# The middle stage's attention values with the value matrix as TensorE's weights: two heads of a pair in the two halves of its columns, and 1/sum spread by TensorE

## The chip, the cores and the metric

One NeuronCore of a Trainium2 chip runs the whole kernel. The metric is the device time of one execution in microseconds. The kernel before has a median of 1403.51 us over three executions (1403.35 to 1405.44).

## The reference

For 16 batches of 112 tokens (width 256) and 375 context tokens, two gated layers of attention and feed-forward follow each other. The change touches the second attention ("large heads", 16 heads of 64) alone:

```
q = ln(x) @ Wq;  k, v = split(concat([ln(ctx), ln(x)]) @ Wkv)       # 112 queries, 487 keys
weight = softmax(where(mask, q k^T / 8, -max))                       # per head, 112 x 487
out = weight @ v                                                     # per head, 112 x 64
x = x + tanh(g) * (out as 112 x 1024) @ Wout
```

After it come a layer norm, a router that picks two of eight experts for each token, and the experts' feed-forward.

## The kernel before

The program has three stages, one after the other: small heads and a first feed-forward (to about 484 us), large heads (`phase_attention_large_heads`, to about 1194 us), and the experts. Products are made in three fp16 passes (`PASSES`: high by high, high by low, low by high) of operands that are split into a high and a low half, so each logical matrix product is three matmuls.

The middle stage runs 16 bodies, one for each batch `b`, of 16 steps `s`. Every engine has its own program with the same steps, and semaphores tie them. Work of several batches lies in one body:

- `scores`: at steps 0, 1, 3, ... 13 PE makes the scores of two heads (six matmuls, which alternate between the two halves of PE's rows; the first pair at step 0). DVE adds the mask and takes the minimum (`maxima`, L1808), ACT makes the exponential with its row sum (L1682) and then the fp16 high half (L1707), and DVE for even heads (L1813) and POOL for odd ones (L1315) subtract to get the low half.
- SP turns a head's `halves` into `pT` (keys on partitions) with a transposing DMA (`turn`, L1236), three steps after the head. `pT` and `halves` have room for `TURN` = 8 heads.
- `values` (L1601): at each step PE multiplies one head, `LAG` = 5 steps behind. The weights are a 128x112 block of probabilities (four blocks of keys; read as 128 columns), the moving operand is the head's 64 columns of `v_s`, so the output is queries by head columns in `ps_o`, eight heads to a bank, 12 matmuls a head.
- `item`: the products for the next batch, one at each step (L1493): eight of keys (`k_s`, six matmuls of 487 columns), eight of values (`v_s`, six of 512 columns), and two of queries (24 of 112 columns). They alternate between two PSUM banks; ACT copies the high half and DVE subtracts for the low half, and an item waits until the one before the last is read.
- One more bank, `ps_x`, is lent by step (`XSLOT`, `lend`): to the previous batch's tail (`h`), to the transposes of the batch after next (`n`), to the router's ranks (`r`) and to the query items (`q`). Each tenant waits until the one before has been read.

The tail of a batch before the change: `out_heads` on DVE takes the reciprocals of eight heads' sums and multiplies a bank of `ps_o` by them (L1823) into `o_n`; `hitem` 0 and 1 are four fp32 transposes each into `ps_x` (L1536), an ACT copy to the high half of `oT` (L1675) and a DVE subtraction for the low half (L1829). Then comes the product with `Wout` (`H_O`, 24 matmuls of 256 columns), the norm, the transposes `H_X` and the router's `H_G`. In the step of a body PE's order is: scores, item, what `XSLOT` has, values.

## Time and profile before

| | us |
|---|---|
| median of three executions | 1403.51 |
| the profiled execution | 1406.79 |
| its span, in which the trace counts | 1405.0 |
| PE, DVE, ACT, POOL busy | 1225.0, 1083.2, 999.4, 813.3 |

Engines: PE is TensorE's matmuls and PEld its weight loads, DVE is VectorE, ACT ScalarE, POOL GpSimd, SP SyncE. A row's matmuls last longer than the distance between their starts, since they are pipelined, so PE's work is read here as the time from the start of one group to the start of the next.

### The profile page before, as it was taken

To read this page: it belongs to the slowest core of one execution; us is meant where nothing else is said; L and a number is where in the kernel's file an instruction comes from. 1 tells how busy PE (TensorE), PEld (TensorE's weight loads), DVE (VectorE), ACT (ScalarE), POOL (GpSimd) and SP (SyncE) were. 2 spreads that over 40 slices of the span, in tenths; PEclk is the share of its full clock that TensorE was granted. 3 is DMA by queue.
4 is the path that set the end of the run, shared out by engine and by line. 5 is a ranking of instruction groups with operands and counts; after the bars stand their busy time and mean duration, and the time that the engine had idled before them with its cause. 6 is when DMAs were issued, how large, how long until landed. Compare 5 with 4: busy or idle time off the path is not lost. (4 is left out here: it accounts for less than half of the span.)

```text
span 1405.0 us, 38066 instructions
## 1 busy us (share of the span) xinstructions
PE 1225.0 (87%) x13060; PEld 880.3 (63%) x13060; DVE 1083.2 (77%) x3112; ACT 999.4 (71%) x2552; POOL 813.3 (58%) x1204
## 2 busy tenths in 40 slices
PE   3999999999986499999999999999999974489994
PEld 1777777777764245566656566656666653389894
DVE  3799999999985168888888888888888882477872
ACT  2888888888883358877787887787888771256562
POOL 3544444444454346677777777777777674146564
PEclk7799999999987599999999999999999985699997
DMA  5444545455420148877788777878777793854333
GB/s 162 131 146 144 148 120 169 114 151 155 134 50 7 49 94 156 141 147 146 153 158 160 143 146 154 147 151 163 152 144 152 137 196 61 316 154 60 57 36 76
DMA packets 309406, 185.50 MB, mean 132 GB/s; under 512 B 257930, under 2 KB 295186, under 8 KB 306112
## 3 DMA queue, kind: packets, MB, share of 16 engines
q1 hardware_dynamic: 293024, 140.82, 47.3%
q0 software_dynamic: 13168, 35.80, 10.5%
q10 hardware_dynamic: 3024, 6.47, 1.5%
q8 instruction: 106, 1.74, 0.5%
q14 instruction: 84, 0.69, 0.2%
HBM read 76.19 MB, written 49.94 MB: 90 GB/s over the span
## 5 line engine op out<-in xcount | busy, mean ns | idle before, releaser
L1682 ACT ACTIVATE b_prob<-b_prob,b_top 112x487 f32<-112x487 f32 x256 | 178.9, 699 | 28.3 <-DVE b_top L1808 26.5
L1315 POOL TENSOR_TENSOR b_halves<-b_prob,b_halves 112x487 f16<-112x487 f32 x128 | 146.9, 1148 | 83.7 <-ACT b_halves L1707 82.2
L1493 PE MATMUL b_ps_p<-w_s,b_tok_s 128*128 128x512 f16 (+1 forms) x768 | 187.7, 381 | 4.0 <-DVE b_k_s L1795 3.2
L1493 PE MATMUL b_ps_p<-b_tok_s,w_s 128*128 128x487 f16 x768 | 181.9, 374 | 6.6 <-POOL b_tok_s L1309 3.7
L1808 DVE CUSTOM_DVE_ANT_0 b_prob<-b_ps_s,b_keep 112x487 f32<-112x487 f32 x256 | 167.3, 655 | 13.2 <-PE b_ps_s L1586 11.6
L717 ACT ACTIVATE a_prob<-a_prob,a_top 112x375 f32<-112x375 f32 x256 | 154.8, 605 | 3.7 <-DVE a_top L853 2.0
L1707 ACT ACTIVATE b_halves<-b_prob 112x487 f16<-112x487 f32 x256 | 156.0, 609 | 0.6
L853 DVE CUSTOM_DVE_ANT_0 a_prob<-a_ps_s,a_keep 112x375 f32<-112x375 f32 x256 | 138.1, 540 | 21.7 <-PE a_ps_s L610 21.4
L618 PE MATMUL a_ps_t<-a_const,a_prob 112*125 112x112 f32 x768 | 135.7, 287 | 10.6 <-ACT a_prob L717 9.1
L1601 PEld LDWEIGHTS b_ps_o<-b_v_s,b_pT 128*128 128x128 f16 (+1 forms) x3072 | 123.9, 99 | 31.4 <-DMA b_pT<-b_halves 11.6
L1601 PE MATMUL b_ps_o<-b_v_s,b_pT 128*128 128x64 f16 (+1 forms) x3072 | 135.0, 195 | 9.2 <-DMA b_pT<-b_halves 9.1
L858 DVE TENSOR_TENSOR a_pT<-a_ps_t,a_pT 125x336 f16<-125x336 f32 x256 | 128.1, 500 | 19.2 <-ACT a_pT L724 18.7
L618 PEld LDWEIGHTS a_ps_t<-a_const,a_prob 112*125 112x125 f32 x768 | 117.5, 196 | 36.1 <-ACT a_prob L717 28.1
L1493 PEld LDWEIGHTS b_ps_p<-b_tok_s,w_s 128*128 128x128 f16 x768 | 66.0, 98 | 95.1 <-issue 20.3
L1493 PEld LDWEIGHTS b_ps_p<-w_s,b_tok_s 128*128 128x128 f16 (+1 forms) x768 | 70.7, 105 | 83.5 <-DVE b_k_s L1795 12.5
L1795 DVE TENSOR_TENSOR b_k_s<-b_ps_p,b_k_s 128x487 f16<-128x487 f32 x128 | 84.5, 661 | 49.9 <-ACT b_k_s L1663 49.9
L1813 DVE TENSOR_TENSOR b_halves<-b_prob,b_halves 112x487 f16<-112x487 f32 x128 | 120.9, 945 | 0.0
L724 ACT ACTIVATE a_pT<-a_ps_t 125x336 f16<-125x336 f32 x256 | 113.5, 443 | 2.3 <-PE a_ps_t L618 2.2
L1670 ACT ACTIVATE b_v_s<-b_ps_p 128x512 f16<-128x512 f32 (+1 forms) x128 | 76.2, 595 | 53.1 <-PE b_ps_p L1493 52.1
L1803 DVE TENSOR_TENSOR b_v_s<-b_ps_p,b_v_s 128x512 f16<-128x512 f32 (+1 forms) x128 | 87.9, 686 | 31.7 <-ACT b_v_s L1670 31.7
L1586 PE MATMUL b_ps_s<-b_k_s,b_q_s 64*112 64x487 f16 x768 | 107.1, 385 | 0.3 <-DVE b_top L1808 0.3
L1663 ACT ACTIVATE b_k_s<-b_ps_p 128x487 f16<-128x487 f32 x128 | 72.8, 570 | 41.6 <-PE b_ps_p L1493 40.2
(263 smaller groups left out, 3022.9 us busy)
## 6 DMA issues: line engine op xcount, KB each, us to landing
xs<-a_blank SPq DMA_DIRECT2D x14, 1032.0 KB, 4.5
c_w_pool<-w_split SPq DMA_DIRECT2D x8, 1600.0 KB, 10.6
b_wch_f<-in_w_experts POOLq DMA_DIRECT2D x32, 384.0 KB, 5.2
w_split<-b_wch_s POOLq DMA_DIRECT2D x32, 384.0 KB, 3.9
a_k_stack<-keys SPq DMA_DIRECT2D x96, 93.8 KB, 3.1
a_ctx_f<-in_ctxT SPq DMA_DIRECT2D x16, 375.0 KB, 3.8
keys<-a_k_s SPq DMA_DIRECT2D x16, 375.0 KB, 3.2
b_ctx_t<-in_ctx SPq DMA_DIRECT2D x16, 375.0 KB
```

Source lines behind the costliest of these rows:

```text
L618: last = pe.transpose(ps_t[h % 2][0:KB0, j * T:(j + 1) * T], prob[:, h % RING, j * KB0:(j + 1) * KB0], ident[0:T, 0:T])
L717: act.activation(prob[:, h % RING, :], prob[:, h % RING, :], ACT.Exp, bias=top[:, h % RING:h % RING + 1], scale=-1.0, accum_out=sums[par][ ...
L724: act.activation(pT[0:KB0, h % RING, HI, :, 0:T], ps_t[h % 2][0:KB0, 0:NB0 * T].rearrange("p (j n) -> p j n", j=NB0), ACT.Copy).then_inc(s ...
L853: dve.tensor_tensor_reduce(prob[:, h % RING, :], ps_s[h % 2][0:T, 0:C], keep[par][:, :], -SCALE0, 3e38, ALU.add, ALU.min, top[:, h % RING: ...
L858: dve.tensor_tensor(pT[0:KB0, h % RING, LO, :, 0:T], ps_t[h % 2][0:KB0, 0:NB0 * T].rearrange("p (j n) -> p j n", j=NB0), pT[0:KB0, h % RIN ...
L1315: pool.tensor_tensor(halves[:, h % TURN, LO, 0:NK], prob[:, h % RING, 0:NK], halves[:, h % TURN, HI, 0:NK], ALU.subtract).then_inc(s_lo[1], 1)
L1493: last = pe.matmul(out, sta(a, k), mov(m, k), start=(k == 0 and n == 0), stop=(k == tiles - 1 and n == 2))
L1601: last = pe.matmul(ps_o[h // 8][:, col:col + D1], pT[0:k, h % TURN, a, j, :], v_s[par][0:k, m, j, h * D1:(h + 1) * D1], start=(h % 8 == 0 ...
L1682: act.activation(prob[:, h % RING, 0:NK], prob[:, h % RING, 0:NK], ACT.Exp, bias=top[:, h % RING:h % RING + 1], scale=-1.0, accum_out=sums ...
L1707: act.activation(halves[:, h % TURN, HI, 0:NK], prob[:, h % RING, 0:NK], ACT.Copy).then_inc(s_hi, 1)
L1808: dve.tensor_tensor_reduce(prob[:, h % RING, 0:NK], ps_s[h % 3][0:T, 0:NK], keep[par][:, :], -SCALE1, 3e38, ALU.add, ALU.min, top[:, h % R ...
L1813: dve.tensor_tensor(halves[:, h % TURN, LO, 0:NK], prob[:, h % RING, 0:NK], halves[:, h % TURN, HI, 0:NK], ALU.subtract).then_inc(s_lo[0], 1)
```

## The change

`values` now takes a pair of heads at each even step, `PAIRLAG` = 6 steps behind. The weights are a head's 128x64 block of `v_s`, the moving operand is the 112 columns of `pT`. The even head is written to partitions 0 to 63 of `ps_o`, then the odd head to 64 to 127, so a bank holds four pairs, already turned (head columns on partitions, queries in the columns). The four-matmul transposes of `o_n` go away. In their place the reciprocals of eight heads are transposed (`H_T`, one transpose to 8x112), scaled by 4096 and split by DVE in two small instructions (`rT`), and multiplied by a 0/1 matrix `picks` (`H_B`, eight matmuls with 8 rows and 112 columns) so that each partition gets its head's reciprocal; ACT copies that to `r_f`; DVE multiplies `ps_o` by it into `o_f`. ACT makes the high half of `oT` from `o_f` (`out_high`), POOL the low half (`out_low`). `XSLOT` has two more slots, 0 and 15. `FREED` counts the semaphore's value after each tail item, since `H_T` raises it twice. The renamed counts in other waits are left out of the diff.

```diff
@@ -1002,7 +1002,8 @@
 KLAST = NK - (NB1 - 1) * KB1
-LAG = 5
+PAIRLAG = 6
+WHOLE = 4096.0
@@ -1059,12 +1060,15 @@
         halves = sb("halves", [T, TURN, 2, NB1 * KB1], F16)
-        pT = sb("pT", [128, TURN, 2, NB1, 128], F16)
+        pT = sb("pT", [128, TURN, 2, NB1, T], F16)
...
         rsum = sb("rsum", [T, H], F32)
-        o_n = sb("o_n", [T, H, D1], F32)
+        picks = sb("picks", [8, 4, 128], F16)
+        rT = sb("rT", [8, 2, T], F16)
+        r_f = sb("r_f", [128, 4 * T], F32)
+        o_f = [sb(f"o_f{i}", [128, 4 * T], F32) for i in range(2)]
@@ -1091,6 +1095,7 @@
         order = sb("order", [T, T], F32)
+        aim = order[0:8, 0:8].rearrange("p (j n) -> p j n", j=4)
@@ -1172,9 +1177,13 @@
-        H_T, H_O, H_X, H_G, HI_ = 0, 2, 3, 4, 5
+        H_T, H_B, H_O, H_X, H_G, NH = (0, 2), (1, 3), 4, 5, 6, 7
+        FREED = (2, 3, 5, 6, 7, 8, 9)
+        HF = FREED[-1]
+        A_B, A_O, AH = (1, 3), (2, 4), 5
         ROUTE = 7
-        NCONST2 = 6
+        NCONST2 = 8
@@ -1184,8 +1193,8 @@
-        XSLOT = {1: ("h", 0), 2: ("r", 0), 3: ("q", 0), 4: ("q", 1), 6: ("h", 1), 8: ("n", 0), 9: ("h", 2), 10: ("n", 1), 11: ("n", 2),
-                 13: ("h", 3), 14: ("h", 4)}
+        XSLOT = {0: ("h", H_B[0]), 1: ("h", H_T[1]), 2: ("r", 0), 3: ("q", 0), 4: ("q", 1), 5: ("h", H_B[1]), 8: ("n", 0), 9: ("h", H_O),
+                 10: ("n", 1), 11: ("n", 2), 13: ("h", H_X), 14: ("h", H_G), 15: ("t", H_T[0])}
@@ -1222,18 +1231,18 @@
...
-                need_all(sp, settled, (s_lo[h % 2], H // 2, b, h // 2 + 1), (s_pv, H, b, h - TURN + 1),
+                need_all(sp, settled, (s_lo[h % 2], H // 2, b, h // 2 + 1), (s_pv, H // 2, b, (h - TURN) // 2 + 1),
                          (s_turned[h % RING], 16 * (H // RING), b, 16 * (h // RING)))
-                sp.dma_start(pT[:, h % TURN, :, :, 0:T].rearrange("p s j n -> p (s j) n"),
+                sp.dma_start(pT[:, h % TURN, :, :, :].rearrange("p s j n -> p (s j) n"),
@@ -1270,9 +1279,8 @@
             pool.memset(halves[:, :, :, NK:NB1 * KB1], 0.0).then_inc(s_zero, 1)
-            pool.memset(pT[:, :, :, :, T:128], 0.0).then_inc(s_zero, 1)
@@ -1315,12 +1323,23 @@
+            def out_low(c, i):
+                need(pool, s_hhi, AH, c, A_O[i], settled)
+                pool.tensor_tensor(oT[:, LO, 4 * i:4 * i + 4, :], o_f[i][:, :].rearrange("p (j n) -> p j n", j=4), oT[:, HI, 4 * i:4 * i + 4, :],
+                                   ALU.subtract).then_inc(s_olo, 1)
...
+                pool.iota(aim, [[2, 4], [1, 2]], base=0, channel_multiplier=-1, allow_small_or_imprecise_dtypes=True).then_inc(s_const2, 1)
+                pool.wait_ge(s_const2, 1)
+                pool.tensor_scalar(picks[:, :, :].rearrange("p j (o n) -> p j o n", o=2), aim.unsqueeze(3).to_broadcast([8, 4, 2, 64]),
+                                   0.0, None, ALU.is_equal).then_inc(s_const2, 1)
+                pool.wait_ge(s_const2, 2)
...
                 pool.iota(token[:, :], [[0, 1]], base=0, channel_multiplier=1, allow_small_or_imprecise_dtypes=True).then_inc(s_const2, 1)
-                pool.wait_ge(s_const2, 3)
+                pool.wait_ge(s_const2, 5)
@@ -1443,6 +1462,8 @@
                     if not first(b):
+                        if s in (3, 7):
+                            out_low(b - 1, s // 7)
@@ -1530,21 +1553,27 @@
             def hitem(c, k):
-                if k < H_O:
-                    for n in range(4):
-                        j = 4 * k + n
-                        last = pe.transpose(ps_x[:, n * T:(n + 1) * T], o_n[:, 2 * j:2 * j + 2, :].rearrange("p h d -> p (h d)"), ident[0:T, 0:T])
+                if k in H_T:
+                    i = H_T.index(k)
+                    need(pe, s_rsum, 2, c, i + 1)
+                    last = pe.transpose(ps_x[0:8, 0:T], rsum[:, 8 * i:8 * i + 8], ident[0:T, 0:T])
+                elif k in H_B:
+                    if first(c):
+                        pe.wait_ge(s_const2, NCONST2)
+                    for j in range(4):
+                        for part in (HI, LO):
+                            last = pe.matmul(ps_x[:, j * T:(j + 1) * T], picks[:, j, :], rT[:, part, :], start=(part == HI), stop=(part == LO))
                 elif k == H_O:
-                    need(pe, s_hhi, 3, c, 2)
-                    need(pe, s_hfree, HI_, c, 2)
+                    need(pe, s_hhi, AH, c, A_O[1])
+                    need(pe, s_olo, 2, c, 2)
@@ -1556,7 +1585,7 @@
                 if not first(b):
-                    need(pe, s_hfree, HI_, b - 1, nh)
+                    need(pe, s_hfree, HF, b - 1, FREED[nh])
@@ -1566,9 +1595,9 @@
                 elif kind == "h":
-                    if k < H_O:
-                        need(pe, s_oread, 2, b - 1, k + 1)
                     hitem(b - 1, k)
+                elif kind == "t":
+                    hitem(b, k)
@@ -1587,21 +1616,24 @@
-            def values(b, par, h):
-                need(pe, s_turned[h % RING], 16 * (H // RING), b, 16 * (h // RING + 1))
-                if h == 0:
+            def values(b, par, pair):
+                for h in (2 * pair, 2 * pair + 1):
+                    need(pe, s_turned[h % RING], 16 * (H // RING), b, 16 * (h // RING + 1))
+                if pair == 0:
...
                     need(pe, s_ifree, PI, b, PI)
-                if h % 8 == 0:
-                    need(pe, s_oread, 2, b - 1, h // 8 + 1)
-                col = (h % 8) * D1
-                for j in range(NB1):
-                    k = rows_of(j)
-                    for n, (a, m) in enumerate(PASSES):
-                        last = pe.matmul(ps_o[h // 8][:, col:col + D1], pT[0:k, h % TURN, a, j, :],
-                                         v_s[par][0:k, m, j, h * D1:(h + 1) * D1],
-                                         start=(h % 8 == 0 and j == 0 and n == 0),
-                                         stop=(j == NB1 - 1 and n == 2), skip_group_check=True)
+                if pair % 4 == 0:
+                    need(pe, s_hfree, HF, b - 1, FREED[H_B[pair // 4]])
+                cols = slice((pair % 4) * T, (pair % 4 + 1) * T)
+                for half in range(2):
+                    h = 2 * pair + half
+                    for j in range(NB1):
+                        k = rows_of(j)
+                        for n, (a, m) in enumerate(PASSES):
+                            last = pe.matmul(ps_o[pair // 4][64 * half:64 * half + 64, cols], v_s[par][0:k, m, j, h * D1:(h + 1) * D1],
+                                             pT[0:k, h % TURN, a, j, :], start=(pair % 4 == 0 and j == 0 and n == 0),
+                                             stop=(j == NB1 - 1 and n == 2), skip_group_check=True)
@@ -1624,11 +1656,12 @@
                         lend(b, par, s)
-                    if not (first(b) and s < LAG):
-                        values(*behind(s, LAG, b, par))
+                    if s % 2 == 0 and not (first(b) and s < PAIRLAG):
+                        c, p, h = behind(s, PAIRLAG, b, par)
+                        values(c, p, h // 2)
@@ -1640,17 +1673,17 @@
             run_batches(pe, body)
-            for h in range(H - LAG, H):
-                values(B - 1, 1, h)
-            need(pe, s_hfree, HI_, B - 1, 0)
+            need(pe, s_hfree, HF, B - 1, FREED[0])
+            hitem(B - 1, 1)
+            for pair in range((H - PAIRLAG) // 2, H // 2):
+                values(B - 1, 1, pair)
+            need(pe, s_hfree, HF, B - 1, FREED[1])
@@ -1665,17 +1698,22 @@
...
             def hitem(c, k):
-                if k < H_O:
-                    need(act, s_hitem, HI_, c, k + 1)
-                    act.activation(oT[:, HI, 4 * k:4 * k + 4, :], ps_x[:, 0:4 * T].rearrange("p (j n) -> p j n", j=4), ACT.Copy).then_inc(s_hhi, 1)
+                if k in H_B:
+                    need(act, s_hitem, NH, c, k + 1)
+                    act.activation(r_f[:, :], ps_x[:, 0:4 * T], ACT.Copy).then_inc(s_hhi, 1)
+            def out_high(c, i):
+                need(act, s_hfree, HF, c, FREED[H_B[i]])
+                need(act, s_hitem, NH, c - 1, H_O + 1)
+                act.activation(oT[:, HI, 4 * i:4 * i + 4, :], o_f[i][:, :].rearrange("p (j n) -> p j n", j=4), ACT.Copy).then_inc(s_hhi, 1)
@@ -1732,6 +1770,8 @@
                         normalise(b + 2)
+                    if not first(b) and s in (2, 7):
+                        out_high(b - 1, s // 7)
@@ -1767,13 +1807,16 @@
             weigh(B - 2)
-            for k in range(HI_):
+            for i in range(2):
+                hitem(B - 1, H_B[i])
+                out_high(B - 1, i)
+            for k in range(H_O, NH):
@@ -1813,36 +1856,41 @@
-            def out_heads(c, par, i):
+            def shares(c, par, i):
...
                 need(dve, s_exp, H, c, 8 * i + 8)
+                need(dve, s_hitem, NH, c - 1, H_T[i] + 1)
                 dve.reciprocal(rsum[:, heads], sums[par][:, heads]).then_inc(s_rsum, 1)
-                need(dve, s_rsum, 2, c, i + 1)
-                need(dve, s_pv, H, c, 8 * i + 8)
-                need(dve, s_hitem, HI_, c - 1, i + 1)
-                dve.tensor_tensor(o_n[:, heads, :], ps_o[i][0:T, :].rearrange("p (h d) -> p h d", h=8),
-                                  rsum[:, heads].unsqueeze(2).to_broadcast([T, 8, D1]), ALU.mult).then_inc(s_oread, 1)
...
             def hitem(c, k):
-                if k < H_O:
-                    need(dve, s_hhi, 3, c, k + 1)
-                    dve.tensor_tensor(oT[:, LO, 4 * k:4 * k + 4, :], ps_x[:, 0:4 * T].rearrange("p (j n) -> p j n", j=4), oT[:, HI, 4 * k:4 * k + 4, :], ALU.subtract).then_inc(s_hfree, 1)
+                if k in H_T:
+                    need(dve, s_hitem, NH, c, k + 1)
+                    dve.tensor_scalar(rT[:, HI, :], ps_x[0:8, 0:T], WHOLE, None, ALU.mult).then_inc(s_hfree, 1)
+                    need(dve, s_hfree, HF, c, FREED[k] - 1)
+                    dve.scalar_tensor_tensor(rT[:, LO, :], ps_x[0:8, 0:T], WHOLE, rT[:, HI, :], ALU.mult, ALU.subtract).then_inc(s_hfree, 1)
+                elif k in H_B:
+                    i = H_B.index(k)
+                    need(dve, s_hitem, NH, c, k + 1)
+                    need(dve, s_olo, 2, c - 1, i + 1)
+                    need(dve, s_hhi, AH, c, A_B[i])
+                    need(dve, s_pv, H // 2, c, 4 * i + 4)
+                    dve.scalar_tensor_tensor(o_f[i][:, :], ps_o[i][:, 0:4 * T], 1.0 / WHOLE, r_f[:, :], ALU.mult, ALU.mult).then_inc(s_hfree, 1)
@@ -1885,27 +1933,27 @@
                             item(b + 1, 1 - par, k)
-                    kind, k = XSLOT.get(s - 1, ("", 0))
+                    kind, k = XSLOT.get((s - 1) % H, ("", 0))
...
                         item(b + 1, 1 - par, ITEMS.index((kind, k)))
-                    if kind == "h" and not first(b):
+                    if kind in ("h", "t") and not first(b):
...
                     if not first(b):
-                        if s == 5:
-                            out_heads(b - 1, 1 - par, 1)
+                        if s == 0:
+                            shares(b - 1, 1 - par, 1)
...
                             norm_x3(b - 1)
-                    if s == 14:
-                        out_heads(b, par, 0)
+                    if s == 10:
+                        shares(b, par, 0)
@@ -1914,11 +1962,13 @@
             run_batches(dve, body)
+            hitem(B - 1, H_T[0])
...
             combine_weights(B - 2)
+            shares(B - 1, 1, 1)
+            hitem(B - 1, H_B[0])
             ranks(B - 2)
-            out_heads(B - 1, 1, 1)
-            for k in range(H_X):
+            for k in range(H_T[1], H_X):
...
```

## Rows read from the trace of the kernel before

**Rows 1.** Windows: one body, the last body, the tail. Length, busy of PE, PEld, DVE, ACT, POOL; PE clock; DMA share; GB/s.
```profile
798.00:840.00 42.00, 40.84 (x440) 25.64 (x436) 34.92 (x88) 34.00 (x81) 31.43 (x51) 1.00 0.82 150
...
1132.00:1172.00 40.00, 25.86 (x342) 19.13 (x338) 28.15 (x72) 23.34 (x54) 28.18 (x51) 0.76 0.91 176
1172.00:1184.00 12.00, 6.72 (x31) 5.86 (x31) 2.57 (x7) 0.90 (x2) 3.93 (x7) 0.64 0.10 29
```

**Rows 2.** Timeline of PE through one body: start us, length us, engine, line, what, count.
```profile
801.12 1.41 PE L1493 MATMUL b_ps_p<-b_tok_s,w_s 128*128 128x487 f16 x6 [0.20 <-DVE b_v_s L1803]
802.37 0.55 PE L1536 MATMUL b_ps_x<-b_const,b_o_n 112*128 112x112 f32 x4
802.75 0.52 PE L1601 MATMUL b_ps_o<-b_v_s,b_pT 128*128 128x64 f16 x12
803.11 1.40 PE L1493 MATMUL b_ps_p<-b_tok_s,w_s 128*128 128x487 f16 x6
805.23 0.21 PE L1613 MATMUL b_ps_x<-b_both,b_before 112*112 112x8 f16 x1 [0.72 <-DVE b_oT L1829]
...
805.36 0.51 PE L1601 MATMUL b_ps_o<-b_v_s,b_pT 128*128 128x64 f16 x12
805.80 0.83 PE L1586 MATMUL b_ps_s<-b_k_s,b_q_s 64*112 64x487 f16 x6
806.56 1.41 PE L1493 MATMUL b_ps_p<-b_tok_s,w_s 128*128 128x487 f16 x6
807.80 1.36 PE L1493 MATMUL b_ps_x<-b_tok_s,w_s 128*128 128x112 f16 x24
809.00 0.52 PE L1601 MATMUL b_ps_o<-b_v_s,b_pT 128*128 128x64 f16 x12
809.36 1.40 PE L1493 MATMUL b_ps_p<-b_tok_s,w_s 128*128 128x487 f16 x6
...
822.32 1.47 PE L1493 MATMUL b_ps_p<-w_s,b_tok_s 128*128 128x512 f16 x6
823.63 2.78 PE L1493 MATMUL b_ps_x<-w_s,b_oT 128*112 128x256 f16 x24
826.25 0.52 PE L1601 MATMUL b_ps_o<-b_v_s,b_pT 128*128 128x64 f16 x12
...
837.05 0.44 PE L1493 MATMUL b_ps_x<-b_wr_s,b_x3T 128*112 128x8 f16 x6
837.35 0.51 PE L1601 MATMUL b_ps_o<-b_v_s,b_pT 128*128 128x64 f16 x12
...
842.94 0.38 PE L1493 MATMUL b_ps_p<-b_tok_s,w_s 128*128 128x487 f16 x1 [0.20 <-DVE b_v_s L1803]
```

**Rows 3.** Timeline of PE, 0.1 us inside one group of six score matmuls.
```profile
812.24 0.62 PE L1586 MATMUL b_ps_s<-b_k_s,b_q_s 64*112 64x487 f16 x4
```

**Rows 4.** Timeline of PE and DVE around step 0 of a body.
```profile
798.41 1.41 PE L1493 MATMUL b_ps_p<-b_tok_s,w_s 128*128 128x487 f16 x6
...
798.52 0.67 DVE L1808 CUSTOM_DVE_ANT_0 b_prob<-b_ps_s,b_keep 112x487 f32<-112x487 f32 x1 [0.59 <-PE b_ps_s L1586]
...
799.11 1.36 DVE L1813 TENSOR_TENSOR b_halves<-b_prob,b_halves 112x487 f16<-112x487 f32 x1
...
799.66 0.52 PE L1601 MATMUL b_ps_o<-b_v_s,b_pT 128*128 128x64 f16 x12
...
800.39 0.68 DVE L1803 TENSOR_TENSOR b_v_s<-b_ps_p,b_v_s 103x512 f16<-103x512 f32 x1
```

**Rows 5.** Groups by line and shape, 620 to 1150 us: busy us, mean ns, idle before.
```profile
L1315 POOL TENSOR_TENSOR b_halves<-b_prob,b_halves 112x487 f16<-112x487 f32 x102 | 116.6, 1143 | 50.3 <-ACT b_halves L1707 49.1
...
L1813 DVE TENSOR_TENSOR b_halves<-b_prob,b_halves 112x487 f16<-112x487 f32 x103 | 98.0, 951 | 0.0
...
L1829 DVE TENSOR_TENSOR b_oT<-b_ps_x,b_oT 128x448 f16<-128x448 f32 x26 | 16.0, 615 | 0.3 <-ACT b_oT L1675 0.3
...
L1675 ACT ACTIVATE b_oT<-b_ps_x 128x448 f16<-128x448 f32 x26 | 13.9, 533 | 0.0
```

More of the change, by code:

```diff
@@ L1210, in _ @@
         def _(sp):
-            settled = (s_zero, 8)
+            settled = (s_zero, 7)
             def load_tokens(c):
@@ L1478, in _ @@
             send_rows(B - 2)
+            for i in range(2):
+                out_low(B - 1, i)
             deviation3(B - 1)
@@ L1545, in hitem @@
                 else:
-                    need(pe, s_hhi, 3, c, 3)
-                    need(pe, s_hfree, HI_, c, H_X + 1)
+                    need(pe, s_hhi, AH, c, AH)
+                    need(pe, s_hfree, HF, c, FREED[H_X])
                     last = product(ps_x[0:T, 0:E], lambda a, t: x3T[:, a, t, :], lambda a, t: wr_s[:, a, t, :])
@@ L1642, in _ @@
             run_batches(pe, body)
-            for h in range(H - LAG, H):
-                values(B - 1, 1, h)
-            need(pe, s_hfree, HI_, B - 1, 0)
+            need(pe, s_hfree, HF, B - 1, FREED[0])
[3 more added lines that the diff above has]
+            need(pe, s_hfree, HF, B - 1, FREED[1])
             ranks(B - 2)
             need(pe, s_rank, 1, B - 1, 0)
-            for k in range(HI_):
-                if k < H_O:
-                    need(pe, s_oread, 2, B - 1, k + 1)
-                need(pe, s_hfree, HI_, B - 1, k)
+            for k in range(2, NH):
+                need(pe, s_hfree, HF, B - 1, FREED[k - 1])
                 hitem(B - 1, k)
-            need(pe, s_hfree, HI_, B, 0)
+            need(pe, s_hfree, HF, B, 0)
             ranks(B - 1)
@@ L1667, in item @@
                     j, half = n // 2, n % 2
-                    need(act, s_pv, H, c - 1, 0)
+                    need(act, s_pv, H // 2, c - 1, 0)
                     r = rows_of(j)
@@ L1769, in _ @@
             weigh(B - 2)
-            for k in range(HI_):
+            for i in range(2):
+                hitem(B - 1, H_B[i])
+                out_high(B - 1, i)
+            for k in range(H_O, NH):
                 hitem(B - 1, k)
@@ L1775, in _ @@
         def _(dve):
-            settled = (s_zero, 8)
+            settled = (s_zero, 7)
             def stats(c):
@@ L1834, in hitem @@
                     dve.scalar_tensor_tensor(x3[:, :], ps_x[0:T, 0:D], tanhs[0:T, 1:2], x_res[:, :], ALU.mult, ALU.add).then_inc(s_hfree, 1)
-                    need(dve, s_hfree, HI_, c, k + 1)
+                    need(dve, s_hfree, HF, c, FREED[k])
                     dve.bn_stats(bns3[:, :], x3[:, :]).then_inc(s_stats3, 1)
@@ L1906, in body @@
                             stats(b + 2)
-            dve.wait_ge(s_zero, 8)
+            dve.wait_ge(s_zero, 7)
             stats(0)
```

25 lines of the change are left out of this document (12 added, 13 removed).

## The prediction

> **What bounds the kernel now.** I read the page first for the shares of the engines, then windows of one body each, then PE's timeline through a body, because a share of busy time doesn't say which engine sets the pace. In the windows the reader is to see that a body of the middle stage has PE busy for all but about 1 us at full clock, and DVE, ACT and POOL for 35, 34 and 31 of 42 us [rows 1]. In the timeline he is to see that PE's groups follow each other with hardly a gap. From one body's first product to the next body's is 842.94 - 801.12 = 41.82 us [rows 2]. Add up what PE has to issue in it, each as the distance to the next start: eight key products of 1.24, eight value products of 1.31, two query items of 1.20, eight groups of scores of 0.76, sixteen heads of values of 0.36 (and 0.08 more for the eight that scores follow: 0.44), the output product 2.62, two groups of output transposes of 0.38, the router 0.30 [rows 2]. That is 9.92 + 10.48 + 2.40 + 6.08 + 5.76 + 0.64 + 2.62 + 0.76 + 0.30 = 38.96. The short groups that are left (five, none longer than the 0.38 of the output transposes) I put at 1.2. So about 40.2 us are work and 1.6 are gaps. The largest is at the ranks: the product at 803.11 is through at 804.35, the ranks start at 805.23, so 0.88 us in which PE waits for DVE's read of `ps_x`. PE sets the pace of bodies 0 to 14. What lengthens PE's issue lengthens the kernel, and what is taken from DVE is worth something only in those 1.6 us.
>
> The last body has no products for a next batch. There PE is busy 25.9 of 40 us at a mean clock of 0.76 and the DMA engines 0.91 [rows 1], so PE doesn't set the pace there.
>
> **The values themselves.** Before, a head is 12 matmuls with 64 moving columns, and takes 0.36 us, 30 ns each [rows 2]. After, it is still 12, but 112 columns move. The row for that width is the query item: 24 matmuls of 112 columns in 1.20 us, 50 ns each [rows 2]. A pair then takes 24 x 0.050 = 1.20 instead of 0.72: +0.48 us. The two heads come one after the other, each twelve matmuls accumulate in one half, so I count no overlap but the last against the first.
>
> Are the weight loads hidden? A group with 8 moving columns and loads of 112 columns takes 0.30 us for six, 50 ns each [rows 2]; so a load of 112 columns needs at most 50 ns, one of 64 columns, at the same 0.45 ns a column, 29 ns. That lies under 50 ns of streaming if it can run while the matmul before it streams. It can with half the rows: the first four score matmuls span 0.62 us and all six 0.83 [rows 2, 3], so the third pair adds 0.21, which is 487 columns and nothing for a load. The output product, loads of 112 columns beside 256 moving ones, shows it for the whole array: 2.62 / 24 = 0.109 us. For half the columns no row shows it. Taken as hidden; the other end is 24 x 0.029 = +0.69 us a pair.
>
> The Trainium skill speaks against the change here: "TensorEngine Tiling (Array Packing)", Restrictions and Gotchas, says that column tiling excludes the fast weight load, and "TensorE: Matmul & The Clock Gate", LDWEIGHTS, prices a load at columns / 1.2 ns. That is 53 ns for 64 columns; the pair would be paced by loads, 1.28 us and not 1.20, and the kernel 9 us longer, as an estimate by that page. The 112-column loads of the row above would be 93 ns by that rule and are at most 50 here, so the trace disagrees with it.
>
> **Changing the way the array is divided.** Values followed by scores cost 0.08 more than values followed by a product, and of the six scores' 0.76 only 3 x 0.21 = 0.63 is streaming, so 0.13 goes before the next whole-array group can start [rows 2, 3]. Until now values were whole-array work; now each pair is entered from a product or a tail item. One more change of division for each pair, 0.08 to 0.13: I take 0.09. Leaving it for scores is already in the 0.08 before. At step 14 no scores follow, which is 0.13 once a body. A pair costs +0.48 + 0.09 = +0.57 us.
>
> Body 0 holds five pairs and bodies 1 to 14 eight each, 117 in all: 117 x 0.57 = +66.7, and 15 x 0.13 = +2.
>
> **Reciprocals in place of transposes.** Two groups of four transposes go: -0.76 us a body [rows 2]. Added are two single transposes (about 0.10 each, a quarter of the 0.38) and two groups of eight matmuls of 112 columns (0.40 each by the query item): 1.00, so +0.24. Both have few rows or columns; if each is a division of the array of its own, entering and leaving adds 0.21 four times, +1.1 in all. Between the two I take +0.65; fourteen bodies have them: +9.
>
> **The other engines.** DVE loses two multiplications of a bank and two subtractions of 0.615; it gains two multiplications of 448 columns (by the 128x448 row 0.615 each) and four instructions on 8 x 112 (about 0.2 each by their size, an estimate from the 0.67 for 487 columns). That is roughly even to -0.5 us. ACT gets two copies more, 2 x 0.533 = 1.1; POOL two subtractions of 448 columns, about 1.143 x 448 / 487 = 1.05 each, 2.1 a body [rows 5]. With 34 and 31 busy of 42 [rows 1] both stay under PE, hidden behind its products; without that cover ACT's would cost 1.1 and POOL's 2.1 us a body. POOL's have a side effect: DVE's subtraction of the low half takes 0.951 on the mean, and 1.36 where it began during one of POOL's [rows 4, 5]. The SP queue gets no transfer more. `turn` waits for a pair instead of a head, still three steps before it is due, and the second head of a pair is used five steps behind as now.
>
> **Where PE will wait.** `H_B` at slot 0 needs `ps_x` read by the two instructions of `H_T` from slot 15, which DVE has in step 0 behind `maxima`, a low half and the last value item. In the trace the scores of step 0 end by 798.41; DVE's three take until 800.39 + 0.68 = 801.07; PE is through with its product at 799.66 [rows 4]. With two small instructions behind, PE would stand from 799.66 to about 801.6: 1.9 us, or 1.5 with the mean low half. What is late next is the pair of values at step 0, behind the waiting `H_B` in PE's queue, and the scores of step 1. Slot 4 (the second query item) follows slot 3 with only a product of 1.24 between, since values have left the odd steps, while the read of the first needs 0.533 + 0.615 and about 0.3 of signalling [rows 5]: 0.2. On the other side values of 1.2 us before every odd step's scores give DVE and ACT time to free the two banks, which takes away part of the present 1.6. I put the net at +1.0 us a body, +14 for fourteen; the ends are -1.6 (all gaps close) and +1.9.
>
> **The last body and the tail.** Eleven pairs lie there, where PE has 14 us idle. At the tail two transposes' round trips are replaced by one through `r_f`, `out_high` and POOL's `out_low`. I take +3, from 0 to +8.
>
> **Sum.** 66.7 + 2 + 9 + 14 + 3 = +94.7. The profiled execution would go from a span of 1405.0 to 1499.7 (1406.79 to 1501.5). Its 1406.79 is 3.3 above the median shown; the difference is added to the median: 1403.51 + 94.7 = 1498.
>
> **Rivals.**
> - The gaps close (DVE and the banks are no longer late) and dividing the array is cheap: 117 x 0.56 + 3 - 22 = +46, 1450 us. For it: DVE has less to do and more time. Against it: slot 0 is a new wait in which nothing helps. Chance 0.12 for 1448 to 1475.
> - The weight loads of half the columns don't hide: +0.69 x 117 = +80, 1578 us. For it: no row shows that division. Against it: it hides with half the rows. Chance 0.06.
> - New waits feed on each other: a long low half beside POOL's new subtractions, `H_B` late, scores late, exponentials late. With every dear end, 117 x 0.61 + 2 + 15 + 27 + 8 = +123, 1527 us, and beyond. Chance 0.06 for above 1525.
> - It gets faster: the upper half's twelve matmuls stream beside the lower half's. A pair then takes 0.60 + 0.09 = 0.69, less than the 0.72 of before, and with the gaps closed the sum is -3.5 + 2 + 9 + 3 - 22 = -12, about 1392 us. It decides from a pair below 0.72 + 0.07 = 0.79 us. For it: the scores' two row halves do stream together, six matmuls in 0.76 against 6 x 0.21. Against it: there the instructions alternate between the halves, here twelve for one half stand in line before the other's first. Chance 0.04. The Trainium skill recommends just this swap: "TensorEngine Tiling (Array Packing)", Performance Considerations, has stationary and streaming operands swapped with two column tiles where the moving side is 64 or less, for up to twice the speed; no run here shows it yet.
> - That nothing changes would need PE to have more than 4 us of slack a body; it has 1.6. Chance 0.01.
>
> **How the numbers follow.** 0.71 for my case, 1475 to 1525, whose likeliest time is 1498. The range reaches down to the closed gaps and up to the dear ends: 1448 to 1530, which leaves out the unhidden loads, the faster case and the far end of the waits, some 0.12 to 0.15. A measurement here tells about 0.2% (3 us) from no change. Faster 0.04, same 0.01, slower 0.95.
>
> **What would show it.** A head's twelve value matmuls at 0.60 us and a pair at 1.20 from start to start; a body of about 47.5 to 48 us between first products; a gap at slot 0 before `H_B` of 1.5 to 1.9 us ending on DVE; POOL at about 33 us a body and ACT at 35; the PE clock still 1.00. A pair under 0.8 or over 1.4 us, or a body bound by DVE's chain rather than PE's issue, would make the prediction wrong.

## The result

The changed kernel takes 1515.16 us (median of four executions, 1512.65 to 1522.98) against 1404.2: ratio 1.0799, 95% interval 1.0757 to 1.084. It is slower by 111 us; 1498 was forecast, with 1448 to 1530 as the range. The profiled execution is the longest of the four, 1522.98 us with a span of 1521.2, so the trace has 116.2 us more than that of before.

Windows of single bodies of the changed kernel, from one set of spreading matmuls of slot 0 to the next, and at the end the last body (columns as in [rows 1]):

```profile
600.55:648.54 47.99, 44.79 (x444) 27.58 (x444) 34.58 (x92) 34.57 (x80) 33.67 (x53) 1.00 0.69 132
...
746.08:795.59 49.51, 46.31 (x444) 28.66 (x445) 34.66 (x92) 34.57 (x80) 33.65 (x53) 0.97 0.65 127
...
845.19:896.22 51.03, 47.94 (x445) 29.16 (x445) 34.69 (x92) 34.57 (x80) 33.67 (x53) 0.93 0.66 124
...
1244.66:1290.00 45.34, 32.38 (x378) 25.02 (x379) 25.65 (x72) 24.51 (x56) 31.70 (x52) 0.73 0.64 132
```

The bodies come in three lengths. The first kind, 48.0 us at full clock, is the one that the prediction described (47.5 to 48), but only two of the twelve distances between the first thirteen output products are of it. In seven the mean granted clock is 0.97 and in three 0.93, and these are 1.5 and 3.0 us longer, with the same number of instructions. DVE, ACT and POOL are busy for 34.7, 34.6 and 33.7 us in each kind, further from the length of the body than before [rows 1].

PE's timeline through a body, the lines that answer to [rows 2]:

```profile
800.95 1.40 PE L1516 MATMUL b_ps_p<-b_tok_s,w_s 128*128 128x487 f16 x6
802.82 0.21 PE L1645 MATMUL b_ps_x<-b_both,b_before 112*112 112x8 f16 x1 [0.47 <-DVE b_rT L1870]
...
807.35 1.40 PE L1516 MATMUL b_ps_p<-b_tok_s,w_s 128*128 128x487 f16 x6
808.90 1.36 PE L1516 MATMUL b_ps_x<-b_tok_s,w_s 128*128 128x112 f16 x24
810.19 1.20 PE L1634 MATMUL b_ps_o<-b_pT,b_v_s 128*64 128x112 f16 x24
811.32 0.83 PE L1615 MATMUL b_ps_s<-b_k_s,b_q_s 64*112 64x487 f16 x6
812.08 1.41 PE L1516 MATMUL b_ps_p<-b_tok_s,w_s 128*128 128x487 f16 x6
813.42 0.56 PE L1565 MATMUL b_ps_x<-b_rT,b_picks 8*128 8x112 f16 x8
813.92 1.41 PE L1516 MATMUL b_ps_p<-b_tok_s,w_s 128*128 128x487 f16 x6
...
838.50 1.20 PE L1634 MATMUL b_ps_o<-b_pT,b_v_s 128*64 128x112 f16 x24
839.63 1.50 PE L1516 MATMUL b_ps_p<-w_s,b_tok_s 128*103 128x512 f16 x6
840.97 0.26 PE L1559 MATMUL b_ps_x<-b_const,b_rsum 112*8 112x112 f32 x1
841.15 0.83 PE L1615 MATMUL b_ps_s<-b_k_s,b_q_s 64*112 64x487 f16 x6
841.91 1.41 PE L1516 MATMUL b_ps_p<-b_tok_s,w_s 128*128 128x487 f16 x6
845.19 0.86 PE L1565 MATMUL b_ps_x<-b_rT,b_picks 8*128 8x112 f16 x8 [1.87 <-DVE b_rT L1870]
845.98 2.08 PE L1634 MATMUL b_ps_o<-b_pT,b_v_s 128*64 128x112 f16 x24
847.99 1.47 PE L1615 MATMUL b_ps_s<-b_k_s,b_q_s 64*112 64x487 f16 x6
849.39 2.62 PE L1516 MATMUL b_ps_p<-b_tok_s,w_s 128*128 128x487 f16 x6
```

What to see: a pair of value matmuls takes 811.32 - 810.19 = 1.13 us to the scores, 24 x 47 ns, and 0.09 before it, since the 24 matmuls of the query item start at 808.90 and are through at 810.10 (1.20, as from 807.80 to 809.00 in [rows 2]). At slot 0 the product begins at 841.91 and is through 1.24 later at 843.15; the spreading matmuls start at 845.19. That is a gap of 2.04 us. From there on everything takes nearly twice as long: 24 value matmuls 2.01 us instead of 1.13, the scores 1.40 instead of 0.76. PE's clock has fallen from its higher level (1.00, 2.4 GHz) to the lower one (0.50, 1.2 GHz), as the window over these groups shows in its third number from the end (columns as in [rows 1]):

```profile
845.40:852.00 6.60, 6.60 (x46) 3.77 (x44) 3.46 (x11) 1.72 (x4) 1.64 (x1) 0.50 0.35 68
```

After 852.1 it is back. In the bodies that are 1.5 us longer the low stretch is about half as long.

DVE around that gap, which answers to [rows 4]:

```profile
842.02 0.67 DVE L1851 CUSTOM_DVE_ANT_0 b_prob<-b_ps_s,b_keep 112x487 f32<-112x487 f32 x1 [1.61 <-PE b_ps_s L1615]
...
842.61 1.45 DVE L1856 TENSOR_TENSOR b_halves<-b_prob,b_halves 112x487 f16<-112x487 f32 x1
...
843.98 0.68 DVE L1846 TENSOR_TENSOR b_v_s<-b_ps_p,b_v_s 103x512 f16<-103x512 f32 x1
...
844.59 0.25 DVE L1868 TENSOR_SCALAR b_rT<-b_ps_x 8x112 f16<-8x112 f32 x1
844.87 0.26 DVE L1870 SCALAR_TENSOR_TENSOR b_rT<-b_ps_x,b_rT 8x112 f16<-8x112 f32 x1
```

The order is as read before: the minimum, a low half that takes 1.45 beside POOL's, the last value item, and only then the two small instructions that PE waits for, the last done at 845.13.

### The profile page after: what moved, and what is told of

It reads as the page before. It is cut to its first block and busy times, and to the rows that moved or that the text cites. A ratio compares the mean times of both kernels' runs of the same rounds, so it can differ in the third digit from the quotient of the medians.

```text
span 1521.2 us, 38714 instructions
## 1 busy us (share of the span) xinstructions
PE 1313.5 (86%) x13220; PEld 925.1 (61%) x13220; DVE 1079.4 (71%) x3144; ACT 1011.4 (66%) x2584; POOL 853.3 (56%) x1237
## 5 line engine op out<-in xcount | busy, mean ns | idle before, releaser
L1323 POOL TENSOR_TENSOR b_halves<-b_prob,b_halves 112x487 f16<-112x487 f32 x128 | 143.5, 1121 | 173.8 <-ACT b_halves L1745 173.8
L1516 PE MATMUL b_ps_p<-b_tok_s,w_s 128*128 128x487 f16 x768 | 189.9, 388 | 3.8 <-POOL b_tok_s L1317 3.7
L1634 PE MATMUL b_ps_o<-b_pT,b_v_s 128*64 128x112 f16 (+1 forms) x3072 | 164.3, 222 | 2.6 <-DMA b_pT<-b_halves 2.6
L1634 PEld LDWEIGHTS b_ps_o<-b_pT,b_v_s 128*64 128x64 f16 (+1 forms) x3072 | 144.7, 115 | 27.1 <-issue 22.2
L1516 PEld LDWEIGHTS b_ps_p<-b_tok_s,w_s 128*128 128x128 f16 x768 | 69.4, 101 | 103.1 <-issue 42.9
L1615 PE MATMUL b_ps_s<-b_k_s,b_q_s 64*112 64x487 f16 x768 | 113.0, 403 | 0.0
L1856 DVE TENSOR_TENSOR b_halves<-b_prob,b_halves 112x487 f16<-112x487 f32 x128 | 109.8, 858 | 0.3 <-ACT b_halves L1745 0.2
```

The costliest lines, as they stand in the source:

```text
L1323: pool.tensor_tensor(halves[:, h % TURN, LO, 0:NK], prob[:, h % RING, 0:NK], halves[:, h % TURN, HI, 0:NK], ALU.subtract).then_inc(s_lo[1], 1)
L1516: last = pe.matmul(out, sta(a, k), mov(m, k), start=(k == 0 and n == 0), stop=(k == tiles - 1 and n == 2))
L1615: last = pe.matmul(ps_s[(2 * pair + half) % 3][0:T, 0:NK], q_s[par][rows, a, pair, :], k_s[par][rows, m, pair, :], start=(n == 0), stop=(n ...
L1634: last = pe.matmul(ps_o[pair // 4][64 * half:64 * half + 64, cols], v_s[par][0:k, m, j, h * D1:(h + 1) * D1], pT[0:k, h % TURN, a, j, :], ...
```

## The experiments

Times are medians, each compared with the kernel before on the same chip. Waits are given as the time from the end of one group to the start of the next, the end being the start plus the group's usual length. "A body" is the distance between two output products (`H_O`) in the trace: 41.81 us before, 48.0 after in bodies without a fall of the clock.

**1. Where the wait at slot 0 leads.**

```diff
                 for s in range(H):
+                    if s == 0 and not first(b):
+                        hitem(b - 1, H_T[0])
                     maxima(b, par, s)
...
-                    if kind in ("h", "t") and not first(b):
+                    if kind == "h" and not first(b):
                         hitem(b - 1, k)
```

> Edit: in step 0 VectorE reads the transposed reciprocals (two small instructions) before anything else, instead of behind the minimum, a low half and a value item; nothing else. Theory A (TensorE's issue sets the pace, and the 2.03 us gap before the spreading matmuls at slot 0 is pure loss, with the fall of the granted clock to 1.2 GHz that follows it in most bodies): the gap goes, a body without a fall goes from 48.0 to about 46.1 us, the bodies of 49.5 and 51 us disappear, the clock stays 1.00; 14 bodies x 1.9 = 27 us plus some 13 to 20 us of clock, so about 1475 us. Theory B (VectorE's chain sets the pace): the wait comes back at the next tenants of the lent bank, the body stays near 48 us, and only the clock's share (13 to 20 us) comes back, about 1500 us.

1477.2 us, ratio to before 1.0527 (1.0509 to 1.0544). A body is 46.54 us, all of them alike, clock 1.00. PE's timeline:

```profile
826.81 1.41 PE L1516 MATMUL b_ps_p<-b_tok_s,w_s 128*128 128x487 f16 x6
828.15 0.56 PE L1565 MATMUL b_ps_x<-b_rT,b_picks 8*128 8x112 f16 x8
...
831.88 1.40 PE L1516 MATMUL b_ps_p<-b_tok_s,w_s 128*128 128x487 f16 x6
834.25 0.21 PE L1645 MATMUL b_ps_x<-b_both,b_before 112*112 112x8 f16 x1 [0.97 <-DVE b_rT L1870]
```

The gap at slot 0 is gone (826.81 + 1.24 = 828.05, start at 828.15, the 0.10 being the change of division). But the ranks now stand at 834.25, 1.13 us after the product before them was through at 833.12, where it was 802.82 - 802.19 = 0.63. So of 2.04 us a body 1.46 came back. The time is that of theory A, and a part of theory B is true: half a microsecond of the wait moved on to the next tenant of the lent bank.

**2. Values ahead of the wait.**

```diff
-                    if s in XSLOT:
+                    if s in XSLOT and s > 0:
                         lend(b, par, s)
                     if s % 2 == 0 and not (first(b) and s < PAIRLAG):
                         ...
+                    if s == 0:
+                        lend(b, par, s)
```

> Edit: at step 0 TensorE does the pair of values before the spreading matmuls instead of behind them, so the 2.03 us gap is filled with 1.2 us of work that was queued behind the wait; VectorE's order is that of the change. Theory A (the gap costs its own length, and the clock falls because of it): the gap shrinks to about 0.8 us, a body takes 46.8 us, no fall of the clock, about 1515 - 17 - 13 = 1485 us. Rival (the clock falls for another reason than this gap, such as the narrower value matmuls): bodies of 1.5 us more stay, about 1498 us.

1489.4 us, ratio 1.0615 (1.0597 to 1.0633). A body is 47.27 us and the clock stays 1.00. The gap at slot 0 is 0.80 us (the values start at 832.08 and are through 1.13 later, the spreading matmuls start at 834.01); the one at the ranks grew to 1.07. The time is nearer to theory A's 1485 than to the rival's 1498: the clock's share comes back even though the wait is only shortened.

**3. Filling the gap with useless work.** The nine matmuls go to a bank that nobody reads.

```diff
+                    if s == 0 and not first(b) and ahead(b, 1):
+                        for _ in range(9):
+                            pe.matmul(ps_s[2][:, 0:NK], wkv_s[:, HI, 0, 0:128], tok_s[1 - par][:, HI, 0, 0:NK], start=True, stop=True)
                     if s in XSLOT:
                         lend(b, par, s)
```

> Edit to the changed kernel: TensorE does nine matmuls of 487 columns into a free bank, read by nobody, at slot 0 before the spreading matmuls, where it stands still for 2.03 us; their 9 x 0.203 = 1.83 us fit into the gap, VectorE's order and all waits are those of the change. Theory A (the clock falls because TensorE stands still for these 2 us): bodies stay at 48.0 us, those of 49.5 and 51 us disappear, the clock is 1.00 and the time is about 1500 us although more is computed. Rival (the clock falls for what the bodies compute, not for the gap): bodies of 49.5 and 51 us stay, 1515 us. If the nine delay what follows, bodies are above 48.1 us.

1499.4 us, ratio 1.0674 (1.0653 to 1.0695). All bodies from the second output product on are 48.00 us. PE's timeline at slot 0, and the window over eleven bodies:

```profile
835.86 2.02 PE L1659 MATMUL b_ps_s<-b_tok_s,w_s 128*128 128x487 f16 x9
837.90 0.56 PE L1565 MATMUL b_ps_x<-b_rT,b_picks 8*128 8x112 f16 x8
...
550.00:1100.00 550.00, 533.87 (x5212) 325.69 (x5211) 395.94 (x1029) 396.12 (x916) 380.29 (x586) 1.00 0.68 131
```

The clock is 1.00, and VectorE's order and the length of the undisturbed body are those of the change. More computed, and 15.7 us less than the change: this is the price of the clock in the median, shown apart from the price of the wait.

**4. Alternating the two halves.**

```diff
-                for half in range(2):
-                    h = 2 * pair + half
-                    for j in range(NB1):
-                        k = rows_of(j)
-                        for n, (a, m) in enumerate(PASSES):
+                for j in range(NB1):
+                    k = rows_of(j)
+                    for n, (a, m) in enumerate(PASSES):
+                        for half in range(2):
+                            h = 2 * pair + half
                             last = pe.matmul(...)
```

> Edit: the 24 value matmuls of a pair alternate between the lower and the upper half of the columns instead of 12 and then 12; same matmuls, same waits. Theory A (the two column halves can stream side by side when their instructions alternate, as the row halves do in the scores): a pair takes about 0.6 instead of 1.13 us, 0.5 x 8 = 4.2 us less a body, about 117 x 0.5 = 60 us less, 1455 us. Rival B (matmuls of different column halves still follow one another, 47 ns each): a pair stays at 1.13 us and the time at 1515 us. Rival C (they collide in the one PSUM bank that both write): a pair takes longer than 1.13 us.

1469.5 us, ratio 1.0469 (1.0451 to 1.0486).

```profile
796.63 1.41 PE L1516 MATMUL b_ps_p<-b_tok_s,w_s 128*128 128x487 f16 x6
797.97 0.78 PE L1634 MATMUL b_ps_o<-b_pT,b_v_s 128*64 128x112 f16 x24
798.68 0.83 PE L1615 MATMUL b_ps_s<-b_k_s,b_q_s 64*112 64x487 f16 x6
...
822.94 1.41 PE L1516 MATMUL b_ps_p<-b_tok_s,w_s 128*128 128x487 f16 x6
826.22 0.56 PE L1565 MATMUL b_ps_x<-b_rT,b_picks 8*128 8x112 f16 x8 [1.86 <-DVE b_rT L1870]
```

A pair takes 798.68 - 797.97 = 0.71 us instead of 1.13: the column halves do stream side by side when their instructions alternate. It is 24 x 30 ns, which is what 12 matmuls of 64 columns cost before (0.36 a head); two halves that shared their streaming fully would need half of 1.13, 0.56. A body without a fall of the clock is 45.24 us, 2.76 less, where 8 x 0.42 = 3.4 left PE's work; the rest went into longer waits. So theory A holds in kind, and its 1455 us were too low. At slot 0 the gap is still 2.04 (822.94 + 1.24 = 824.18, start 826.22), and five of twelve bodies are 46.6 to 46.9 us long, with the clock at its lower level for a part; in the change it was ten of twelve behind the same gap.

**5. Both.**

> Edit: the two edits of e1_early_read and e2_alternate together. If both theories A hold, a body has about 48.0 - 1.9 - 4.2 = 41.9 us, as the kernel before (41.8), and the time is about 1415 us; if the column halves stream together but VectorE, ScalarE or the banks cannot follow a shorter TensorE, the body ends near 43 to 44 us with waits for the key and value items, about 1435 us; if the halves don't stream together it equals e1_early_read.

1437.6 us, ratio 1.0255 (1.023 to 1.028). A body is 44.02 us, clock 1.00 throughout.

```profile
813.48 1.40 PE L1516 MATMUL b_ps_p<-b_tok_s,w_s 128*128 128x487 f16 x6
816.27 0.21 PE L1645 MATMUL b_ps_x<-b_both,b_before 112*112 112x8 f16 x1 [1.39 <-DVE b_rT L1870]
...
829.33 1.41 PE L1516 MATMUL b_ps_p<-b_tok_s,w_s 128*128 128x487 f16 x6
831.54 1.47 PE L1516 MATMUL b_ps_p<-w_s,b_tok_s 128*128 128x512 f16 x6 [0.80 <-DVE b_k_s L1838]
```

Neither 41.9 nor 1415: the second branch of the expectation. PE's work is now about 0.6 us above that of before (values 8 x 0.71 + 7 x 0.09 = 6.3 against 6.4, and the reciprocals' 0.7), but the ranks wait 816.27 - 814.72 = 1.55 us and the first value item 831.54 - 830.57 = 0.97.

**6. The paired schedule by itself, in the kernel before.**

```diff
-                    if not (first(b) and s < LAG):
-                        values(*behind(s, LAG, b, par))
+                    if s % 2 == 0 and not (first(b) and s < 6):
+                        for lag in (6, 5):
+                            values(*behind(s, lag, b, par))
```

> Edit to the kernel before: its values keep their operands and their tail, but TensorE takes two heads one after the other at each even step, six steps behind, as the change does, instead of one at each step. Theory A (the paired schedule itself costs little, the change's loss is the width of the moving operand plus the new waits): waits for the lent bank grow by the 0.36 us of values that no longer stand before them at steps 2, 4 and 10 and the waits for the two product banks shrink, so a body of 41.8 to 42.8 us, 1404 to 1418 us. Rival (the clumped order is what opened the gaps of the change): a body of 43.5 us or more, 1430 us.

1418.4 us, ratio 1.0105 (1.009 to 1.0121); a body is 42.91 us, 1.10 more. It lies just past the upper end of theory A (42.8 us, 1418 us), with operands and tail untouched.

```profile
809.04 1.40 PE L1493 MATMUL b_ps_p<-b_tok_s,w_s 128*128 128x487 f16 x6
811.51 0.21 PE L1613 MATMUL b_ps_x<-b_both,b_before 112*112 112x8 f16 x1 [1.08 <-DVE b_oT L1830]
...
824.36 1.41 PE L1493 MATMUL b_ps_p<-b_tok_s,w_s 128*128 128x487 f16 x6
826.33 1.47 PE L1493 MATMUL b_ps_p<-w_s,b_tok_s 128*128 128x512 f16 x6 [0.56 <-DVE b_k_s L1796]
```

The ranks wait 811.51 - 810.28 = 1.23 (0.88 before), the first value item 826.33 - 825.60 = 0.73: items and tenants of the lent bank that had 0.36 us of values between them now follow each other directly. So the order alone costs the kernel before 1.1 us a body. In the change its share was not measured apart: with the wait at slot 0 gone (experiment 1) the other waits there are about 0.8 us above those of before.

**7. Mending the waits, in both kernels.** In the first, on top of experiment 5, DVE reads the lent bank earlier and ACT copies an item earlier; in the second the same is done to the kernel before. The diff leaves out that these calls are skipped at their old places.

```diff
 # VectorE
                     maxima(b, par, s)
+                    if s in (2, 14) and not first(b):
+                        hitem(b - 1, XSLOT[s - 1][1])
                     if s % 2 == 0 and not (first(b) and s < 2):
                         ...low_half(c, h)
 # ScalarE
+                    if s == 7 and ahead(b, 1):
+                        for k in PSLOT[6]:
+                            item(b + 1, 1 - par, k)
                     exps(...)
```

> Edit: e3_both, and VectorE reads the lent bank in steps 2 and 14 right behind the minimum instead of behind a low half and an item, and ScalarE at step 7 copies the key item before its exponential. Theory A (what is left over the kernel before, 44.02 against 41.81 us a body, is mostly three waits: 1.55 us at the ranks, 0.97 at the first value item, 0.4 at the router): the first two close and the third mostly, a body of 41.6 to 42.2 us, 1400 to 1410 us. Rival (VectorE or ScalarE is at its limit, the waits move on): a body stays above 43 us, 1422 us or more.

1426.5 us, ratio 1.0165 (1.0151 to 1.0179). A body is 43.06, the rival's side of the expectation.

```profile
808.10 1.40 PE L1516 MATMUL b_ps_p<-b_tok_s,w_s 128*128 128x487 f16 x6
809.74 0.21 PE L1645 MATMUL b_ps_x<-b_both,b_before 112*112 112x8 f16 x1 [0.24 <-DVE b_rT L1873]
...
813.85 1.40 PE L1516 MATMUL b_ps_p<-b_tok_s,w_s 128*128 128x487 f16 x6
816.24 1.36 PE L1516 MATMUL b_ps_x<-b_tok_s,w_s 128*128 128x112 f16 x24 [0.99 <-DVE b_q_s L1844]
```

The ranks' wait fell to 809.74 - 809.34 = 0.40, and a new one stands two steps on: the second query item waits 816.24 - 815.09 = 1.15 for DVE's read of the first. That the low half, put off in DVE's program, is the reason is tried in the last run below.

> Edit to the kernel before: the same two changes of order on VectorE and ScalarE as in e6_both_mended, nothing of the change itself. Theory A (TensorE's issue sets the pace of the kernel before, with 1.6 us of gaps a body): the 0.88 us at the ranks and the 0.36 us at the first value item close, a body of 40.6 to 40.9 us, 14 x 1.1 = 15 us less, 1389 us. Rival (the 42 us are set by the engines' chain from scores to scores): 1404 us as before.

1411.7 us, ratio 1.0063 (1.005 to 1.0077): slower than before by a little, a miss for both sides. Most bodies are 42.35 us.

```profile
720.14 0.17 PE L1613 MATMUL b_ps_x<-b_both,b_before 112*112 112x8 f16 x1
...
721.19 0.53 PE L1601 MATMUL b_ps_o<-b_v_s,b_pT 128*128 128x64 f16 x12 [0.82 <-DMA b_pT<-b_halves]
...
805.19 0.17 PE L1613 MATMUL b_ps_x<-b_both,b_before 112*112 112x8 f16 x1
...
807.29 0.53 PE L1601 MATMUL b_ps_o<-b_v_s,b_pT 128*128 128x64 f16 x12 [1.88 <-DMA b_pT<-b_halves]
```

The ranks follow the product at once (it started at 803.95, and 803.95 + 1.24 = 805.19). Then PE stands for the transposed probabilities of the head at step 2: 0.8 to 1.0 us in five of the first thirteen bodies, 0.4 in one, nothing in four, and 1.5 to 2.0 in the three slowest; 805.19 is in the slowest, of 43.10 us. Where it doesn't stand there, as at 677.87, it can stand 1.25 us before the second query item instead. Two more items now wait 0.5 us each (before 711.93 and 738.48) where they had waited 0.1 at most. That the wait at the ranks was closed and others opened for it is seen; that the late low half made the transfer late is read from the code and the releaser, not measured by itself.

A third order, the low half first and then the read ahead of the key item:

> Edit: e6_both_mended, but at step 2 VectorE does the low half first and only then reads the transposed reciprocals, ahead of the key item; step 14 and ScalarE's step 7 as there. In e6_both_mended the low half that was put off came back as a 0.99 us wait before the second query item. Theory A (each wait can be shortened without opening another): ranks' wait from 1.55 to about 0.9 us, no new wait at the query item, a body of 42.3 us, 1412 us. Rival (the order of the paired schedule is tight, one wait for another): a body of 43 us, 1425 us, as e6_both_mended.

1427.2 us, ratio 1.0167 (1.0149 to 1.0185), bodies of 43.05 us with a few of 43.2 and 43.3: the same as the other order, the rival's side. Against the first mended run the wait at the second query item fell from 1.15 to 0.57 us (816.02 - 815.45) and the one at the ranks rose from 0.40 to 0.97 (810.09 - 809.12): what one gained the other lost. No kernel here beats the one before.

## Why the prediction came out as it did

**What the bound is: right for this change, with a limit.** PE's issue sets the pace; a body of 48.0 without a fall of the clock was given as 47.5 to 48. Experiment 4 took 3.4 us of PE's work from a body and 2.8 came back. The limit: PE's gaps are no slack that a better order simply gives back. In the kernel before, the edit that closed the largest one (0.88 at the ranks) made a body 0.5 us longer (experiment 7).

**The values: +3.3 us a body, not +4.7.** The mechanism held (12 matmuls a head of 112 columns, loads hidden, no overlap in this order), its size was off. The pair streams in 1.13 us, 47 ns each, where I took the query item's 50; and nothing more is lost on leaving it, for scores (810.19 to 811.32) or a product (838.50 to 839.63, also 1.13), so the 0.08 before the scores and the 0.13 at step 14 are not there. 8 x 1.13 + 7 x 0.09 = 9.7 against 16 x 0.36 + 8 x 0.08 = 6.4. Entering costs the 0.09 taken. The prediction spoke of 53 ns a load by the Trainium skill, "TensorE: Matmul & The Clock Gate", LDWEIGHTS. The pair disagrees with that too: its matmuls, each with a load of its own, start every 47 ns.

**The reciprocals: about +0.7, as taken (0.65).** The spreading matmuls take 0.49 (813.42 to 813.92) and 0.10 to enter, the single transpose 0.18 (840.97 to 841.15).

**The waits: +2.3 us a body, not +1.0.** The wait at slot 0 was forecast at 1.9 in place and length and is 2.04. What failed is the step "values of 1.2 us before every odd step's scores give DVE and ACT time [...] which takes away part of the present 1.6". Added up as product end to next start, the gaps of a body are 2.04 at slot 0, 0.63 at the ranks, 0.32 at the second query item (808.90 - 808.58), 0.54 at the first value item and 0.45 at the router, 4.0 in all against 1.7 before. Those at the ranks (0.88 before) and at step 1, for DVE's read of a value item (0.26 before), became shorter; those at the second query item, the first value item and the router became longer. Of the net 2.3, experiment 1 gives back 1.5 by an early read at slot 0. For the remaining 0.8 or so experiment 6 shows a cause: the paired order by itself costs 1.1 in the kernel before.

The errors of the two terms nearly cancel: 3.3 + 0.7 + 2.3 = 6.3 for 6.19 measured, 6.34 forecast. That the body was met within 0.15 us is luck: the values were 1.4 us too dear and the waits 1.3 too cheap.

**The clock: not foreseen, 20 us of the trace.** From the first to the thirteenth output product the trace has 595.99 us against 501.91, +94.1; 12 x 6.19 = 74.3 of that are the bodies, 19.8 are ten bodies that grew by 1.5 or 3 us. (Another 6.6 lie before the first of these products.) The prediction said "the PE clock still 1.00". It named the wait of 1.9 us, and put it down at its own length only. Experiments 1, 2 and 3 each shorten or fill it, and in each the clock stays 1.00; with the gap kept and a pair at 0.71 us (experiment 4) half of the falls remain. So the wait is needed for them; its length alone doesn't decide. Behind the same 2.04 us the clock fell in ten of twelve bodies here and in five of twelve in experiment 4; gaps of 1.55 us in every body (experiment 5, ranks) brought no fall, and neither did the single one of 2.02 us in the mended kernel before (experiment 7). What decides is open. The trace is that of the longest execution, with a mean granted clock of 0.925 against 0.934 to 0.936 in the other three, so its 19.8 are more than the 15.7 by which experiment 3 lowers the median. The forecast of 1498 has no term for this; that 1515 still lies in the range is owed to an upper end that was meant for dearer waits.

**The last body and the tail: +8, not +3.** The last three distances between output products sum to 114.7 us against 100.1; one of them is a full body's 6.2, which leaves 8.4. Of this, 1.5 is one more fall of the clock in the first of the three (48.6 us against 41.0) and 7.5 are in the second, which holds the first half of the last body (40.2 against 32.6). In the last body the wait at slot 0 is 3.2 us long and PE runs at a mean clock of 0.73. How the 7.5 divide wasn't tried. The third distance is even 0.5 shorter than before (25.9 against 26.4), though in it the output product waits for POOL, the part which the prediction passed over with "replaced by one through [...] `out_low`":

```profile
1286.34 0.58 ACT L1716 ACTIVATE b_oT<-b_o_f 128x448 f16<-128x448 f32 x1 [0.86 <-DVE b_o_f L1877]
1286.78 0.95 POOL L1436 DMA_INDIRECT xs<-b_xr,b_slot  x1 [0.30 <-issue]
1287.74 2.03 POOL L1329 TENSOR_TENSOR b_oT<-b_o_f,b_oT 128x448 f16<-128x448 f32 x2
...
1289.91 1.50 PE L1516 MATMUL b_ps_x<-w_s,b_oT 128*112 128x256 f16 x6 [5.01 <-POOL b_oT L1329]
```

POOL sends the rows of another batch (two indirect transfers) before it takes the two subtractions, though ScalarE's high half stood at 1286.92. From the last values (through at 1282.9) to the product it is 7.0 us where it was 5.35 (1169.2 to 1174.56 in the trace of before). The last values themselves come 18.9 us after the output product before them, where it was 21.1, so this wait isn't what made the end longer.

**The rivals.** That the gaps close: no. The unhidden loads: no. Faster by streaming the halves together: not in this order, but experiment 4 shows the mechanism, and experiment 5 what it would have been worth: even with it and without the wait at slot 0 the kernel is 2.5% slower than before. The break-even of 0.79 a pair "with the gaps closed" was nearly met (0.71 + 0.09 = 0.80), and the gaps did not close. The Trainium skill, "TensorEngine Tiling (Array Packing)", Performance Considerations, advises to swap the operands and use two column tiles where 64 columns move. Here this gives two heads in 0.71 us against 0.72 unswapped, so nothing, and that only when the instructions alternate.

## What to carry to other kernels

Price a swap of weights and moving operand by the columns that then move: two operands of 64 and 112 columns cost 30 and 47 ns a matmul here, and alternating the halves of the array was needed just to get back to 30. When PE sets the pace, a new wait can cost its length and what the clock loses behind it (here 1.5 and, in the median, another 1.1 us a body), so look for what stands in front of the awaited instruction in its engine's program; reading the lent bank first was one moved line and worth 38 us. Moving a read earlier in a tight static order moves the wait to whatever was put off: measure the body, not the gap.

## What the runs showed of the hardware that I had not expected

- Matmuls of 112 columns into alternating column halves start every 30 ns (a pair in 0.71 us), into one half every 47 ns (1.13 us), with both halves writing the same PSUM bank.
- Behind a PE gap of 2.04 us the clock fell to its lower level in ten of twelve bodies. In three it stayed there for almost 7 us (845.3 to 852.1 in one) and the body grew by 3 us, in seven for about half of that, and it grew by 1.5; nine useless matmuls in the gap made the kernel 16 us faster. One gap of 2.02 us in another kernel brought no fall.
- Leaving work on half the columns for work on half the rows cost nothing that the starts show (a pair takes 1.13 us before scores and before a product), while leaving whole-array work for the scores cost 0.08 (0.44 against 0.36 a head before the change).
